# A twelve-stage network on one core: order of the values, the scores and the first transfers in its two narrow self-attentions

## What is computed

```python
q = (x @ wq).reshape(B, S, 16, 8).transpose(0, 2, 1, 3)
k = (x @ wk).reshape(B, S, 4, 8).transpose(0, 2, 1, 3)
v = (x @ wv).reshape(B, S, 4, 8).transpose(0, 2, 1, 3)
q = q * cos + _rotate_half(q) * sin
k = k * cos + _rotate_half(k) * sin
k, v = jnp.repeat(k, 4, axis=1), jnp.repeat(v, 4, axis=1)
scores = jnp.einsum('bhqd,bhkd->bhqk', q, k) / jnp.sqrt(jnp.float32(8))
scores = jnp.where(causal, scores, -jnp.inf)
attn = jax.nn.softmax(scores, axis=-1)
out = jnp.einsum('bhqk,bhkd->bhqd', attn, v)
return out.transpose(0, 2, 1, 3).reshape(B, S, D) @ wo
```

## Time and profile before

| | |
|---|---|
| median of 3 runs | 2827.16 us (2826.16 to 2830.75) |
| the profiled execution | 2828.28 us, its span 2826.5 us |
| TensorE busy | 2144.6 us (76%), granted clock 0.868 on average |
| VectorE, ScalarE, GpSimd busy | 1688.5 (60%), 1161.8 (41%), 665.6 us (24%) |
| first narrow self-attention | 783 to 1112 us of the span |
| second narrow self-attention | 1915 to 2211 us |

### The profile page before, as it was taken

How to read it: one execution, slowest core, us unless ns; L and a number is a source line. 1 busy time by engine, 2 the same in 40 slices (tenths; PEclk the granted TensorE clock), 3 DMA queues, 4 the chain that set the end, 5 groups by cost and what they waited for, 6 DMA issues and landing times. The chain is left out here.

```text
span 2826.5 us, 36362 instructions
## 1 busy us (share of the span) xinstructions
PE 2144.6 (76%) x11488; PEld 1272.0 (45%) x11488; DVE 1688.5 (60%) x4410; ACT 1161.8 (41%) x2237; POOL 665.6 (24%) x711
## 2 busy tenths in 40 slices
PE   6774796767638887897888998674778796778397
PEld 4562572225512223564444554461233465667254
DVE  3676437979747764545545554354776346456677
ACT  2442337644315554222666767331344322133222
POOL 0430004643210000001655555331222000244000
PEclk7786797988859998898999999785999798689699
DMA  1000000010042200001222321103220001000000
GB/s 35 34 1 6 0 0 5 1 49 1 1 92 44 43 10 1 1 0 62 77 75 79 83 79 43 46 1 56 50 49 1 1 0 63 26 1 1 0 1 15
DMA packets 37757, 79.97 MB, mean 28 GB/s; under 512 B 6912, under 2 KB 21248, under 8 KB 36448
## 3 DMA queue, kind: packets, MB, share of 16 engines
q1 hardware_dynamic: 37344, 77.36, 10.9%
q10 hardware_dynamic: 256, 0.68, 0.1%
HBM read 51.80 MB, written 7.34 MB: 21 GB/s over the span
## 5 line engine op out<-in xcount | busy, mean ns | idle before, releaser
L659 ACT ACTIVATE spt<-P 128x1024 f32<-128x1024 f32 (+3 forms) x256 | 220.9, 863 | 296.4 <-PE P L509 296.1
L2125 PE MATMUL P<-XT,W 128*128 x424 | 220.9, 617 | 61.1 <-ACTq L2159 61.1
L2201 DVE SCALAR_TENSOR_TENSOR X<-P,WE,X 128x128 f32 x576 | 162.3, 344 | 166.6 <-PE P L2142 161.6
L2142 PEld LDWEIGHTS P<-W,e_h 128*128 128x128 f32 (+1 forms) x1952 | 220.4, 190 | 61.0 <-issue 56.0
L2142 PE MATMUL P<-W,e_h 128*128 128x128 f32 (+1 forms) x1952 | 227.5, 277 | 3.4 <-DVE X L2201 3.4
L963 POOL TENSOR_TENSOR d_e<-d_e,d_rc 128x512 f32<-128x512 f32 (+3 forms) x256 | 180.2, 726 | 174.4 <-DVE d_rc L870 141.8
L2170 ACT ACTIVATE e_g<-P 128x512 f32<-128x512 f32 x148 | 88.4, 597 | 311.2 <-PE P L2125 311.2
L524 PE MATMUL P<-spt,sva 128*32 128x512 f32 (+3 forms) x1024 | 213.3, 541 | 0.2 <-POOL spt L697 0.2
L608 DVE TENSOR_REDUCE smf<-P 128x2 f32<-128x1024 f32 x128 | 152.9, 1220 | 86.7 <-PE P L497 84.6
L911 ACT ACTIVATE d_e<-d_e,d_mn 128x512 f32<-128x512 f32 (+3 forms) x256 | 141.7, 554 | 131.2 <-DVE d_mn L862 130.8
L2188 DVE TENSOR_TENSOR e_h<-e_g,P 128x512 f32<-128x512 f32 x148 | 101.6, 687 | 110.4 <-PE P L2128 109.3
(11 more groups left out here) (336 smaller groups left out, 4320.2 us busy)
## 6 DMA issues: line engine op xcount, KB each, us to landing
d_bt<-in_alibi SPq DMA_DIRECT2D x32, 512.0 KB, 3.8
d_moved<-d_raw SPq DMA_DIRECT2D x256, 64.0 KB, 2.0
ska<-parts_k SPq DMA_DIRECT2D x96, 64.0 KB
sqa<-parts_q SPq DMA_DIRECT2D x96, 64.0 KB
W<-in_w_L_xattn SPq DMA_DIRECT2D x1, 4291.0 KB, 13.7
W<-in_w_L_ffn SPq DMA_DIRECT2D x1, 3333.0 KB, 12.2
W<-in_w_L_ffn SPq DMA_DIRECT2D x1, 3155.0 KB, 10.5
parts_k<-sparts SPq DMA_DIRECT2D x8, 384.0 KB, 2.3
```

The costliest lines, as they stand in the source:

```text
L659: a.activation(PT[:, n % 2, :, t, N - late(t):N], P[:, BANK_T:BANK_T + 2, 0:late(t)], ACT.Exp, scale=SC).then_inc(s("exp"), 1)
L2125: pe.matmul(P[:, PG + j % 2, :], w["w1"][:, col:col + 128], x, start=True, stop=True).then_inc(s("gate"), 1)
L2142: last = pe.matmul(P[:, PY + j % 2, 128 * t:128 * (t + 1)], HT[rows, u % 2, blk, 128 * t:128 * (t + 1)], w2, start=n == 0, stop=n == len(p ...
L2201: last = v.scalar_tensor_tensor(x, y, k.WE[:, bass.ds(c * 4 + t, 1), e], x, ALU.mult, ALU.add)
```

## The change

It edits `self_attention` alone, for both calls:

- `values` takes one key tile of two items, four heads on the four column groups, at four places in two steps (PLACES), a step later than before. PT gets a third buffer; OA, OT, R1 and R2 lose their second.
- In a unit `scores` comes last, on TensorE and for `maxima` on VectorE.
- The causal mask is a bf16 constant that TensorE adds to the diagonal block of the scores by an identity matmul, two a unit; VectorE reduces both heads at once in both stages.
- The stacks of batch 0 come in two portions, items 0 and 1 first; the keys' on SP, the queries' on ScalarE's queue. The zero rows go first. The scores of step 2 wait for the second portions. The next stage's weights are loaded after the keys of batch 1 went out.
- ScalarE fills KA in place of GpSimd.

```diff
+    EARLY = 2
+    PLACES = ((0, 1), (0, 3), (1, 1), (1, 2))
...
-        PT, VA = sb("pt", 2, 2, QT, N), sb("va", 2, QT, VH, 32)
+        PT, VA = sb("pt", 3, 2, QT, N), sb("va", 2, QT, VH, 32)
...
-        R1, R2 = sb("r1", 2, N), sb("r2", 2, N)
...
+        R1, R2 = sb("r1", N), sb("r2", N) if rope else None
...
-        MASK, SPENT = (sb("mask", N), sb("spent", 2, 2, N)) if causal else (None, None)
+        MASK = sb("mask", 128, dt=BF16)
...
+        def out_parts(eng, x, b):
+            eng.wait_ge(s("cut_" + x), b + 1)
+            eng.dma_start(scratch[x][128 * b:128 * (b + 1), :], PARTS_OF[:, "kq".index(x)].rearrange("p c n -> p (c n)")).then_inc(s("written_" + x), 16)
+
+        def blank_rows(eng, b):
+
+            eng.wait_ge(s("zero"), 1)
+            for j in range(2):
+                eng.dma_start(QA[64 * j + ROWS:64 * j + 64, b % 2], ZERO[0:64 - ROWS, :].unsqueeze(1).to_broadcast([64 - ROWS, PAIRS, N])).then_inc(
+                    s(f"stack_q{b % 2}" if b else "early_q"), 16)
+
+        def stacked(eng, x, b):
+            y = "kq".index(x)
+            eng.wait_ge(s("written_" + x), 16 * (b + 1))
+            src = scratch[x][128 * b:128 * (b + 1), :].rearrange("(p j d) (c n) -> j c d p n", p=PAIRS, j=2, c=3)
+            for first_, last_ in ((0, EARLY), (EARLY, PAIRS)) if b == 0 else ((0, PAIRS),):
+                for j in range(2):
+                    for c, pair in enumerate(PARTS):
+                        eng.dma_start((KA, QA)[y][64 * j + 8 * c:64 * j + 8 * c + 8, b % 2, first_:last_], src[j, pair[1 - y], :, first_:last_]).then_inc(
+                            s("early_" + x if b == 0 and first_ == 0 else f"stack_{x}{b % 2}"), 16)
+
         @block.sync
         def _(sp):
-            for b in range(B):
-                for y, x in enumerate("kq"):
-                    rows = scratch[x][128 * b:128 * (b + 1), :]
-                    sp.wait_ge(s("cut_" + x), b + 1)
-                    sp.dma_start(rows, PARTS_OF[:, y].rearrange("p c n -> p (c n)")).then_inc(s("written_" + x), 16)
-                    sp.wait_ge(s("written_" + x), 16 * (b + 1))
-                    if b >= 2:
-                        sp.wait_ge(s("score_t"), QT * PAIRS * (b - 1))
-                    elif x == "k":
-                        sp.wait_ge(s("keys_ready"), b + 1)
-                    dst = (KA, QA)[y][:, b % 2]
-                    src = rows.rearrange("(p j d) (c n) -> j c d p n", p=PAIRS, j=2, c=3)
-                    for j in range(2):
-                        for c, pair in enumerate(PARTS):
-                            sp.dma_start(dst[64 * j + 8 * c:64 * j + 8 * c + 8], src[j, pair[1 - y]]).then_inc(s(f"stack_{x}{b % 2}"), 16)
-                        if x == "q":
-                            sp.wait_ge(s("zero"), 1)
-                            sp.dma_start(dst[64 * j + ROWS:64 * j + 64], ZERO[0:64 - ROWS, :].unsqueeze(1).to_broadcast([64 - ROWS, PAIRS, N])).then_inc(s(f"stack_{x}{b % 2}"), 16)
-                if b == 0:
+            blank_rows(sp, 0)
+            blank_rows(sp, 1)
+            out_parts(sp, "k", 0)
+            sp.wait_ge(s("keys_ready"), 1)
+            stacked(sp, "k", 0)
+            for b in range(1, B):
+                out_parts(sp, "k", b)
+                if b == 1:
                     load_weights(k, i + 1)
+                    sp.wait_ge(s("keys_ready"), 2)
+                else:
+                    sp.wait_ge(s("score_t"), QT * PAIRS * (b - 1))
+                    blank_rows(sp, b)
+                stacked(sp, "k", b)
+                out_parts(sp, "q", b)
+                stacked(sp, "q", b)
...
-                if p == 0 and u == 0:
+                if u == 0 and p == 0 and b == 0:
                     for x in "kq":
-                        pe.wait_ge(s(f"stack_{x}{b % 2}"), STACKS[x] * (b // 2 + 1))
+                        pe.wait_ge(s("early_" + x), STACKS[x])
+                elif u == 0 and p == (0 if b else EARLY):
+                    for x in "kq":
+                        pe.wait_ge(s(f"stack_{x}{b % 2}"), STACKS[x] * (b // 2 + 1) - (32 if x == "q" and b % 2 == 0 else 0))
...
-                                     start=True, stop=True)
+                                     start=True, stop=not causal)
+                if causal:
+                    if c == 0:
+                        pe.wait_ge(s("mask"), 1)
+                    for h in range(2):
+                        last = pe.matmul(P[:, BANK_S + 2 * (c % 2) + h, wide(u) - 128:wide(u)], k.identb[:], MASK[:], start=False, stop=True)
...
-            def values(n, tiles):
-                b, p = n // PAIRS, n % PAIRS
-                if tiles[0] == 0:
-                    pe.wait_ge(s("kept" if causal else "exp"), QT * (n + 1))
-                    if p == 0:
-                        pe.wait_ge(s("out_a"), number["v", b][1])
-                    if n >= 2 and n % 2 == 0:
-                        pe.wait_ge(s("copied"), n // 2)
-                for t in tiles:
-                    for h in range(2):
-                        c = 32 * (2 * (n % 2) + h)
-                        last = pe.matmul(P[c:c + 32, BANK_PV, N - late(t):N], VA[:, b % 2, t, (2 * p + h) // vrep, :],
-                                         PT[:, n % 2, h, t, N - late(t):N], start=t == 0, stop=t == QT - 1)
-                if tiles[-1] == QT - 1:
-                    last.then_inc(s("value"), 1)
+            def values(g, t):
+
+                if t == 0:
+                    pe.wait_ge(s("kept" if causal else "exp"), 2 * QT * (g + 1))
+                    if g % GROUPS == 0:
+                        pe.wait_ge(s("out_a"), number["v", g // GROUPS][1])
+                    if g:
+                        pe.wait_ge(s("copied"), g)
+                for h in range(4):
+                    n, c = 2 * g + h // 2, 32 * h
+                    last = pe.matmul(P[c:c + 32, BANK_PV, N - late(t):N], VA[:, g // GROUPS % 2, t, (4 * (g % GROUPS) + h) // vrep, :],
+                                     PT[:, n % 3, h % 2, t, N - late(t):N], start=t == 0, stop=t == QT - 1)
+                last.then_inc(s("value"), 1)
 
             for f in first:
                 other(*f[1:])
-            for n in range(ITEMS + 6):
+            for n in range(ITEMS + 8):
                 for u in range(QT):
-                    if n < ITEMS:
-                        scores(n, u)
                     if 0 <= n - 2 < ITEMS:
                         transposed(n - 2, u)
                     for what, which in step_uses(n, u):
                         other(what, which)
-                    if u % 2 == 1 and 0 <= n - 3 < ITEMS:
-                        values(n - 3, (u - 1, u))
+                    if n >= 4 and n - 4 < ITEMS and (n % 2, u) in PLACES:
+                        values(n // 2 - 2, PLACES.index((n % 2, u)))
+                    if n < ITEMS:
+                        scores(n, u)
...
-                if not causal:
-                    v.tensor_reduce(MF[:, n % 2, u, :], P[:, bank:bank + 2, :], AX.X, ALU.max, negate=True).then_inc(s("max"), 1)
-                    return
-                if c >= 2:
-                    v.wait_ge(s("max"), c - 1)
-                for h in range(2):
-                    last = v.tensor_tensor_reduce(SPENT[:, c % 2, h, 0:wide(u)], P[:, bank + h, 0:wide(u)], MASK[:, N - wide(u):N], -1.0, 3e38,
-                                                  ALU.add, ALU.min, MF[:, n % 2, u, h:h + 1])
-                last.then_inc(s("max"), 1)
+                v.tensor_reduce(MF[:, n % 2, u, :], P[:, bank:bank + 2, 0:wide(u)], AX.X, ALU.max, negate=True).then_inc(s("max"), 1)
...
-                    if n < ITEMS:
-                        maxima(n, u)
                     for what, which in step_uses(n, u):
                         if what not in on_a:
                             other(what, which)
+                    if n < ITEMS:
+                        maxima(n, u)
...
                 a.wait_ge(s("score_t"), QT * n + t + 1)
-                if n >= 2 and t == 0:
-                    a.wait_ge(s("value"), n - 1)
-                a.activation(PT[:, n % 2, :, t, N - late(t):N], P[:, BANK_T:BANK_T + 2, 0:late(t)], ACT.Exp, scale=SC).then_inc(s("exp"), 1)
+                if n >= 3:
+                    a.wait_ge(s("value"), QT * ((n - 3) // 2) + t + 1)
+                a.activation(PT[:, n % 3, :, t, N - late(t):N], P[:, BANK_T:BANK_T + 2, 0:late(t)], ACT.Exp, scale=SC).then_inc(s("exp"), 1)
 
...
             a.activation(k.warm[:], k.ones[0:1, 0:1], ACT.Exp)
+            a.activation(KA[:, 0], k.max_rows.unsqueeze(2).to_broadcast([128, PAIRS, N]), ACT.Copy).then_inc(s("keys_ready"), 1)
+            out_parts(a, "q", 0)
+            stacked(a, "q", 0)
             other("v", 0)
-            for n in range(ITEMS + 6):
-                if n >= 5 and n % 2 == 1 and n - 4 < ITEMS:
-                    copied((n - 4) // 2)
+            a.activation(KA[:, 1], k.max_rows.unsqueeze(2).to_broadcast([128, PAIRS, N]), ACT.Copy).then_inc(s("keys_ready"), 1)
```

(15 more changed lines are left out.)

53 lines of the change are left out of this document (28 added, 25 removed).

## The result

| | before | the change |
|---|---|---|
| median | 2826.66 us (2825.84 to 2830.75) | **2795.06 us** (2792.05 to 2800.16) |
| ratio, 95% interval | | **0.9887**, 0.987 to 0.9905 |
| profiled execution | 2828.28 us, span 2826.5 | 2800.16 us, span 2798.4 |
| TensorE busy, mean granted clock | 2144.6 us, 0.868 | 2137.2 us, 0.851 |

What follows compares the result with a forecast made beforehand. Start waits, then TensorE idling under exponentials and VectorE waiting for it, were taken as the bound. Starts -25.3 and -16.8, loops -32.6 and -13.2 sum to -87.9 us: 2740.4 profiled, median 2739, range 2714 to 2768.

Steps and rivals of the forecast that it cites:

- Starts: Start of both stages: without slow copies and queued queries, first scores come 25.3 and 16.8 us earlier.
- Values of four heads: Both loops: four heads share TensorE's array, so a key tile costs 0.92 us, two pairs 3.7 instead of 7.4.
- 6.66: First loop: us a step without projections, from walking two steps through as 6.40 + 6.92 = 13.32.
- Steps with projections, first loop: First loop: VectorE's operations after each k or q projection add 1.9 us, six times, 11.4 in all.
- TensorE's clock falls: Rival, both loops: less work brings half clock, +33 and +82 us, 2900 in all; chance 0.03.
- The walk: Both loops: two steps timed, each start the later of its engine and its data; 6.66 and 5.8 us a step.
- A projection: Second loop: VectorE work before the last reduction, none hidden, adds 4.6 us, six times.
- A finished batch: Second loop: each finished batch adds 2.5 us, three times, 7.5 in all.
- the forecast's 239.4: Second loop, first score to last addition: 252.6 us less the forecast gain of 13.2.
- The mask: Second loop: TensorE's mask matmuls cost 0.27 us a unit, 1.1 a step; bounds 0.17 and 0.5.
- The rival of 2764: Rival, second loop: changes of tiling mode drain TensorE, 0.5 us a unit, 25 us more in all; chance 0.15.
- 5.8 a step: Second loop: us a step without projections, bound by unit 1's chain, not by an engine; 34 steps.

Runs made afterwards that it cites:

- x15_change_held: The change with 4 matmuls of zeros on TensorE in every step of both stages, nothing else; 2779.3 us, ratio 0.9853.
- x5_hold: The change with 11 matmuls of zeros ahead of TensorE's wait for the maxima in six second-stage steps; 2783.9 us, ratio 0.9862.
- x13_hold_tmask: The change with VectorE's conversions spread and 4 matmuls of zeros a step in the second stage, mask on TensorE; 2763.5 us, ratio 0.9772.
- x12_hold_vmask: The change with, in the second stage, conversions spread, mask back on VectorE and 5 matmuls of zeros a step; 2754.0 us, ratio 0.9736.
- x4_defer: The change with VectorE's conversion work behind each projection spread over the next step's units; 2781.4 us, ratio 0.9852.
- x10_vmask_new: The change with VectorE's conversions spread and the second stage's mask back on VectorE, no zeros; 2798.3 us, ratio 0.9897.
- x7_mix_defer: The change in the first stage; in the second its start, the loop of before and VectorE's conversions spread; 2754.4 us, ratio 0.9761.

## Why the prediction was wrong

- **Starts: right.** -24.2 and -16.8 against -25.3 and -16.8. The late portions and the issues on ScalarE cost nothing that shows.
- **Values of four heads: right in kind.** A tile of four occupies 0.99 us, not 1.84. The estimate from the Trainium skill's figure (page "TensorE: Matmul & The Clock Gate", section "Measured speedup vs the span model") had been 1.16, my row had given 0.92; the trace lies between. Together with the order this makes clean steps of 6.85 instead of 6.66, so 34 x 0.19 = 6.5 of the 14.9 us missing in the first loop.
- **Steps with projections, first loop.** I took 1.9 each, with the clock at 1.00, and that size was right: at the one place where x15_change_held kept it at 1.00 (925.61), the two steps take 8.76 and 6.82, 1.9 above two clean ones. In the change the step after one pays too (8.35 instead of 6.82), TensorE's clock having fallen behind its waits of 1.69 and 1.06 us: 6 x 1.5 = 9 us. With the clean steps that is all of the 14.9.
- **The failed step: "TensorE's clock falls" got a chance of 0.03, because "73% busy for 120 us with the clock at 1.00 in another stage" was to hold for both loops.** It held for neither: the changed first loop was busy 73% of its time too (194.2 of 267.7 us), at a mean clock of 0.91, and the second stood at 0.76. The walk took every row at full clock. In the second loop 38.1 us are missing. Zeros on TensorE alone give back 17.9 (277.5 to 259.6; 10 by the ratios), spreading VectorE's chain as well another 18.8 (240.8; 23 by the ratios, which hold the first loop too). The second share isn't clock alone, but with the chain the clock still fell (0.88, and 0.95 without). The rival as I wrote it, 82 us for the whole second loop at half clock, was not reached.
- **How much of the 38.1 is clock (an estimate from steps at 1.00).** Clean steps take 6.10 instead of 5.8, 10 us in 34. A projection costs 4.2 instead of 4.6: in x5_hold the four steps from 2028.40 take 10.76, 5.68, 10.76 and 5.67, 8.5 above four clean ones. A finished batch costs 2.9 instead of 2.5 (8.96 in x15_change_held). Together these sizes are 9 us; the other 29 I put down to the clock.
- **Luck.** The 240.8 of x13_hold_tmask is within 2 us of the forecast's 239.4, but two errors cancel in it: the clean steps cost those 10 us more, and with the chain spread, which the change doesn't do, a projection costs 3.1 (8.37, 7.02, 8.24 and 7.02 in four steps), 9 us less in six.
- **The mask: right in size.** The mask occupies 0.22 us (2108.43 to 2108.65), the scores ahead of it 0.21 instead of 0.12 in x12_hold_vmask, so 0.31 a unit against 0.27; 10 to 14 us in the whole loop with the clock up. The rival of 2764 had 0.5 a unit; no run shows such a price. The Trainium skill's rule on drains (page "TensorEngine Tiling", section "Key Properties") stood beside that rival; what the trace shows that could be a drain is the 0.09 us of the scores ahead of the mask. But I credited the reduction that it relieves with a shorter loop, and at full clock it is a loss.
- **5.8 a step was compared with the wrong number.** The 7.22 of before was a mean with projections in it. Clean steps of before already alternated between 5.40 and 6.82 late in the loop (mean 6.11) and 5.89 and 6.80 earlier (6.35); the change's 5.94 and 6.26 have a mean of 6.10. There was little to gain but at the projections.

What stays open: what exactly makes the clock fall. It was at half behind the waits of 2.54 us, but in x4_defer it also fell at 1995.1 with no wait of TensorE above 0.98 us in the 8 us before (TensorE had been busy 0.9 of the 2.5 us from 1992.0), and two executions of the same code differ by 0.04 in mean clock. The experiments varied the amount of work, not its spacing.

## What to carry to other kernels

Whoever takes work off TensorE in a loop with short waits should read the granted clock of that loop before and after; busy time doesn't show it. Where it falls, a few matmuls of zeros in the wait are the cheapest test. As a cure they brought the changed loop level with the loop of before with its conversions spread, which needs none. Compare steps of the same kind (clean with clean) when you forecast a loop, and spread one engine's long chain before changing another engine's order.

## What the runs showed of the hardware

- Useless work can pay: 5 matmuls of 512 columns a step raised the loop's mean clock from 0.64 to 0.94 and cut it from 276.7 to 230.8 us (ratio 0.9897 to 0.9736).
- TensorE's busy share didn't tell its clock: 76% of the loop at 0.64 (x10_vmask_new), 79% at 0.94 (x7_mix_defer).
- The same edit, the mask on TensorE, costs 14 us in one loop (mean clock 0.94 without it) and saves 19 in another (0.64 without it); by the ratios 11 and 13.
- A bf16 copy on VectorE takes 0.43 us beside ScalarE's fill of 4096 columns, and took 3.90 (786.79 to 790.69) beside GpSimd's fill of the same tile and the three memsets that GpSimd ran behind it, to 790.84. VectorE's next operation took 4.07 us beside GpSimd's second fill (790.57 to 794.25), and 0.69 later (796.62).
